# A low part, two GpSimd sums and one copy change places in a pipelined transformer kernel

## Time and profile before

| | |
|---|---|
| median of three runs | 924.88 us (922.01 to 927.58) |
| profiled execution | 921.48 us |
| its span, first to last instruction | 919.6 us |
| mean granted clock of PE | 0.966 of 2.4 GHz |
| busy: PE, DVE, ACT, POOL | 88%, 82%, 68%, 19% |
| a body, bodies 3 to 13 | 50.2 us |

### The profile page before, as it was taken

The page is one execution under the profiler, slowest core; times in us unless marked ns, Lnnn a source line. Parts: engine busy times, 40 slices in busy tenths (PEclk is TensorE's granted clock), DMA queues, the critical chain, the costliest instruction groups (busy, mean ns, idle before and its releaser), DMA issues.

```text
span 919.6 us, 18573 instructions
## 1 busy us (share of the span) xinstructions
PE 812.3 (88%) x5962; PEld 694.2 (75%) x5962; DVE 755.9 (82%) x2475; ACT 621.0 (68%) x1279; POOL 172.8 (19%) x160
## 2 busy tenths in 40 slices
PE   2276789999999999999999999999999999998782
PEld 0264668888889787888888888878888888787681
DVE  3648586798989989898989899898989898969565
ACT  1123668786868686877878686868788796777330
POOL 2100002121220403121212113030212121201110
PEclk9687899999999999999999999999999999999986
DMA  6714587667774757675686958486667657572100
GB/s 200 225 65 123 140 192 179 159 147 184 166 183 133 171 142 180 155 168 153 160 180 153 182 135 185 135 182 152 164 150 184 159 135 173 156 174 63 52 34 12
DMA packets 147737, 137.59 MB, mean 150 GB/s; under 512 B 19298, under 2 KB 144803, under 8 KB 147636
## 3 DMA queue, kind: packets, MB, share of 16 engines
q1 hardware_dynamic: 147636, 136.33, 60.6%
HBM read 98.49 MB, written 4.23 MB: 112 GB/s over the span
## 4 chain that ended last, share of the span: by engine, by line
PE 62%; ACT 18%; issue 8%; DVE 6%; SPq 4%; DMA 2%; POOL 1%; POOLq 0%; DVEq 0%; ACTq 0%
PE back_bank L1054 12%; PE turn_bank L1010 9%; PE context_bank L1064 6%; PE score_bank L1112 5%; PE front_bank L1048 5%; PE score_bank L1113 4%; ACT sc L529 4%; PE front_bank L1081 4%; ACT ffT L597 4%; PE back_bank L1034 3%; PE attend_bank L1034 3%; PE back_bank L1025 3%; PE front_bank L1218 2%; SPq L308 2%; ACT L529 2%
## 5 line engine op out<-in xcount | busy, mean ns | idle before, releaser
L529 ACT ACTIVATE sc<-sc,negmax 128x256 f32<-128x256 f32 x512 | 230.4, 500 | 39.0 <-DVE negmax L844 38.5
L844 DVE CUSTOM_DVE_ANT_0 sc<-score_bank,side 128x256 f32<-128x256 f32 x512 | 195.2, 419 | 37.9 <-PE score_bank L1113 34.1
L515 ACT ACTIVATE pt<-turn_bank 128x512 f32<-128x512 f32 x176 | 104.8, 595 | 134.7 <-PE turn_bank L1010 94.7
L1010 PE MATMUL turn_bank<-ident,sc 128*128 128x128 f32 x1024 | 157.2, 276 | 1.3 <-ACT sc L529 1.2
L1010 PEld LDWEIGHTS turn_bank<-ident,sc 128*128 128x128 f32 x1024 | 123.3, 141 | 32.3 <-issue 13.7
L452 POOL TENSOR_TENSOR rstd<-var,half_neg 128x2 f32<-128x2 f32 x64 | 54.3, 848 | 436.6 <-DVE var L773 435.3
L1112 PE MATMUL score_bank<-ks,qs 128*128 128x256 f32 x512 | 122.6, 321 | 8.0 <-DVE negmax L844 6.7
L1054 PE MATMUL back_bank<-w,ffT 128*128 128x256 f32 x512 | 118.0, 379 | 0.0
L1054 PEld LDWEIGHTS back_bank<-w,ffT 128*128 128x128 f32 x512 | 97.0, 190 | 12.7
L1113 PE MATMUL score_bank<-mask_neg,ident_r 128*128 128x512 f32 x256 | 102.1, 399 | 0.0
L1112 PEld LDWEIGHTS score_bank<-ks,qs 128*128 128x128 f32 x512 | 78.3, 192 | 16.7 <-DVE negmax L844 8.9
(11 more groups left out here) (209 smaller groups left out, 1990.0 us busy)
## 6 DMA issues: line engine op xcount, KB each, us to landing
side<-in_side SPq DMA_DIRECT2D x128, 512.0 KB, 5.1
qs<-qh SPq DMA_DIRECT2D x128, 64.0 KB, 4.2
ks<-kh SPq DMA_DIRECT2D x128, 64.0 KB, 3.8
ks<-kl SPq DMA_DIRECT2D x128, 64.0 KB, 4.3
qs<-ql SPq DMA_DIRECT2D x128, 64.0 KB, 4.4
wb<-in_wb SPq DMA_DIRECT2D x16, 512.0 KB, 6.7
xN<-in_x SPq DMA_DIRECT2D x16, 256.0 KB, 4.8
ada<-ada_rows SPq DMA_DIRECT2D x16, 256.0 KB, 4.9
```

The source lines that it names most:

```text
L515: e.activation(pt[:, h % NP2, :, :], two(tbank[h % 2]), ACT.Copy).then_inc(copied[h % 4], 1)
L529: i = e.activation(sc[:, h % NS, q, :], sc[:, h % NS, q, :], ACT.Exp, bias=negmax[:, q, h:h + 1], scale=-1.0)
L844: i = e.tensor_tensor_reduce(sc[:, s % NS, q, :], two(sbank[s % 2])[:, q, :], side[:, (H * X.i + s) % NSIDE, q, :], -1.0, 3.4e38, ALU.add, ...
L1010: i = e.transpose(tbank[h % 2][:, k * S + q * P:k * S + q * P + P], sc[:, h % NS, q, k * P:k * P + P], ident[:, :])
```

## The change

Four places change; no arithmetic does.

1. DVE: `u_l` (L856) moves from the end of slot 1 to slot 0, behind the bias of head 0 and ahead of the norm of layer 0 (L786, L794).
2. POOL: `x2b` (L487) moves from slot 13 of the body in which its sample is in B to slot 1 of the next (its sample is then in T), ahead of that slot's power. It waits for n3 and, where there is an F, for F's y.
3. POOL: `x1res` (L475) moves from slot 14 to slot 13, ahead of that slot's power, and waits for `xa` of G, where there is a G, as `x2b` did before.
4. ACT: in slot 13 the copy of turned head 11 moves ahead of the tanh. In bodies without B there is no tanh in this slot.

```diff
@@ -461,13 +461,20 @@
                         e.wait_ge(ready, 2 + SET0)
                     if is_step(t, s, 1, 0):
                         e.wait_ge(ready, 4 + SET0)
+                    if s == 1 and T:
+                        if F:
+                            e.wait_ge(ev["y_ready"], F.n)
+                        e.wait_ge(ev["n3_ready"], T.n)
+                        e.tensor_tensor(x2b[:, :, :], x2[:, :, :], rows(b2r[:, :]), ALU.add).then_inc(ev["x2b_ready"], 1)
                     if s == 1 and F:
                         power(F, 1, ev["y_var"], ev["y_rstd"])
                     if s == 4 and T:
                         e.wait_ge(ev["bcf_ready"], T.n)
                         e.wait_ge(ev["x3_turned"], T.n)
                         e.tensor_tensor(x3c[:, :, :], x3[:, :, :], rows(bcf[:, :]), ALU.add).then_inc(ev["x3c_ready"], 1)
-                    if s == 14 and F:
+                    if s == 13 and F:
+                        if G:
+                            e.wait_ge(ev["xa_ready"], G.n)
                         wait(e, ev["x2_ready"], F.i - 1)
                         e.wait_ge(ev["x1_ready"], F.n)
                         if t == -1:
@@ -480,11 +487,6 @@
                         power(T, 3, ev["x4_var"], ev["x4_rstd"])
                     if s == 8 and B:
                         power(B, 2, ev["x2_var"], ev["x2_rstd"])
-                    if s == 13 and B:
-                        e.wait_ge(ev["n3_ready"], B.n)
-                        if G:
-                            e.wait_ge(ev["xa_ready"], G.n)
-                        e.tensor_tensor(x2b[:, :, :], x2[:, :, :], rows(b2r[:, :]), ALU.add).then_inc(ev["x2b_ready"], 1)
                     if s == 13 and G:
                         power(G, 0, ev["xa_var"], ev["xa_rstd"])
                     if s == 15 and B:
@@ -605,6 +607,8 @@
                     if s == 12 and G:
                         e.wait_ge(ev["expert_done"], G.n)
                         e.activation(g1[:, :], fbank[:, 0:S], ACT.Identity, bias=wexp[:, A:A + 1]).then_inc(ev["g1_ready"], 1)
+                    if s == 13 and X:
+                        copy_turned(X, s - LT)
                     if s in (11, 12, 13, 14) and B:
                         j = s - 11
                         quarter(e, "u1_ready", B, j)
@@ -613,7 +617,7 @@
                         e.activation(th[:, j % 2, :, :], ffT[:, 2 * j:2 * j + 2, :], ACT.Tanh, scale=0.851).then_inc(ev["th_ready"], 1)
 
                     for x, h in lagging(X, B, s - LT):
-                        if s in ACT_COPIES:
+                        if s in ACT_COPIES and s != 13:
                             copy_turned(x, h)
 
             turns(body)
@@ -845,15 +849,15 @@
                                                        -1.0, 3.4e38, ALU.add, ALU.min, negmax[:, q, s:s + 1])
                         i.then_inc(biased[s % 4], 1)
 
+                    if s == 0 and U:
+                        e.wait_ge(ev["uh_ready"], U.n)
+                        e.tensor_tensor(u_l[:, :, :], t_u[:, :, :], u_h[:, :, :].bitcast(F32), ALU.subtract).then_inc(ev["ul_ready"], 1)
                     if s == 0 and F:
                         norm_scale(F, 0, xa, gamma0[:, :], ev["xa_rstd"], ev["y_scaled"])
                         norm_shift(F, 0, yN, xa, beta0[:, :], ev["y_scaled"], ev["y_ready"])
                     if s == 1 and F:
                         e.wait_ge(ev["y_ready"], F.n)
                         norm_stats(F, 1, yN, ev["y_stats"], ev["y_aggr"], ev["y_var"])
-                    if s == 1 and U:
-                        e.wait_ge(ev["uh_ready"], U.n)
-                        e.tensor_tensor(u_l[:, :, :], t_u[:, :, :], u_h[:, :, :].bitcast(F32), ALU.subtract).then_inc(ev["ul_ready"], 1)
                     if s == 2 and T:
                         e.wait_ge(ev["w2_done"], T.n)
                         e.wait_ge(ev["x2b_ready"], T.n)
```

## The result

The changed kernel takes 900.47 us (median of 4 runs, 899.63 to 902.63); the kernel before, beside it, took 924.75 (4 runs, 922.01 to 927.58). The ratio is 0.9741, 95% interval 0.9707 to 0.9775. The forecast was 900 from 924.88.

The account below looks back on a forecast made before the run. TensorE was taken to bound the kernel, with 1.51 us idle per full body. Gains of 17.3 (u_l), 5.5 (copy), 1.0 and 1.0 (sums at the ends) make 24.8 us, from 924.88 to a forecast of 900, range 893 to 909.

Parts of the forecast that it names:

- issue: Profile's label for TensorE's 1.20 us wait at differ, slot 2, 12 times; read as waiting for u_l, costing 1.44 each.
- full-body term of 1.82: Gain per full body: 1.44 us at differ from moving u_l, 0.38 at slot 14's mix from moving the copy.
- What is late next: Check of body 8, slot 14 through slots 2 to 10, with TensorE and VectorE earlier; claimed nothing binds.
- The sum would be the same: If GpSimd's multiply held L939 in slot 14, total gain unchanged; slot 4's margin shrinks from 0.9 to 0.4 us.
- Rival 2: New wait in slots 3 to 5 takes back about half of the 1.44 us: 908.8 us, 9 in 100.
- I take nothing for the new neighbours: Slot 1: bias of head 1 and statistics beside moved x2b counted as slowed by 0; bound 1.06 us.
- Body 15's 1.0: Gain of 1.0 us in body 15, as neither moved sum would block the norm at L794 there.
- The blocked scale in body 0: F's norm at 66.82, blocked by x1res, takes 1.89 us for 0.88; unblocking it was to win 1.0 us.
- Rival 1: The copy ahead of slot 13's tanh gives nothing at slot 14's mix: 905.6 us, 11 in 100.
- rival 3: Pause at differ in slot 2 stays, being TensorE's own: 917.4 us, 3 in 100.
- rival 4: TensorE's granted clock falls when it works without pauses; slower, 937 us at clock 0.94, 5 in 100.
- Rival 5: No change: pauses come back one for one on VectorE, 82% busy; 924 us, 2 in 100.

Follow-up runs that it names:

- low_copy: Against the kernel before, u_l moves to slot 0 and the copy ahead of the tanh, GpSimd's two sums stay: 923.51 us, ratio 0.9995.
- x1res_14: The changed kernel with the sum x1res alone put back in slot 14: 913.08 us, ratio 0.989 to the kernel before.
- low_only: Against the kernel before, only u_l moves to slot 0; sums and copy stay: 916.2 us, ratio 0.9942.
- clear_ends: The changed kernel with three more GpSimd waits: x3c for the x1 shift, x2b without F for u_l, x1res without G for f: 898.76 us, ratio 0.974.
- low_sums: The changed kernel with the copy of head 11 put back behind the tanh: 904.56 us, ratio 0.979 to the kernel before.
- sums_only: Against the kernel before, only GpSimd's two sums, x2b and x1res, move: 908.77 us, ratio 0.9859.

## Why the prediction was right, and which step of it was wrong

**Right: what bounds the kernel.** "1.51 us of a body is all that a better order can win there" counted idle time alone; with what each stall costs beyond its length (1.44 and 0.38 in all) the working gave 1.82, and 1.83 was measured. TensorE is then busy for the whole body, so this order has no idle time left to win. Reading "issue" as a wait for L856, from the timeline, was right: each kernel that writes `u_l` early enough, by whichever route, has no pause at `differ`.

**Right: the copy.** 0.38 a body with the others (48.76 to 48.37), nothing alone, since TensorE then only waits longer in slot 2. The copy ends at 494.24 and `mix` starts without a wait 0.43 later; with the 0.15 that it needs behind a copy the margin is 0.28, where the working had 0.06. ACT, then PE, body 8 of after (answers to rows 6 and 7):

```profile
493.63 0.61 ACT L517 ACTIVATE pt<-turn_bank 128x512 f32<-128x512 f32 x1
494.11 0.66 ACT L617 ACTIVATE th<-ffT 128x512 f32<-128x512 f32 x1
```

```profile
494.67 1.06 PE L1068 MATMUL context_bank<-pt,vp 128*18 128x256 f32 x16
```

**Wrong: "In the bodies at full load this buys no further time, as the end of `u_l` already left the path; it only widens margins."** Without the sums' move the same two edits buy nothing (low_copy: 50.22). The full-body term of 1.82 had the right size, but was put to two edits that reach it only together with the third: going from low_copy to the change, the sums' move is worth 1.85. The failed step is in "What is late next": it followed TensorE's steps and VectorE's steps, each moved earlier, and asked only which would wait for which. It did not ask what else TensorE's signals start. The turn of x3 starts `x3c` on GpSimd (in the earlier trace rows its releaser stands in the brackets: back_bank L995), and the shift of x1, two SBUF inputs, stood just ahead of it, in the timeline of VectorE before:

```profile
465.75 0.88 DVE L794 SCALAR_TENSOR_TENSOR x<-xa,rstd,ada 128x256 f32<-128x256 f32 x2
```

467.60 - 465.75 = 1.85, a margin of 0.97 beyond the shift's 0.88. Both numbers were there, and the rest is subtraction: with `u_l` early TensorE comes 1.44 sooner, gap 0.41 (measured 0.34); with the copy 1.82 sooner, gap 0.03 (measured 0.03); VectorE 1.06 earlier gives 1.09 (measured 1.05). The change is fast because 1.05 is more than 0.88, by 0.17 us. The cost of a collision was in the earlier trace rows too, 1.0 us. So the forecast number was right in part by luck, with a margin that it didn't know of. Rival 2 (9 in 100) named the right stretch; where it comes true, without the sums' move, its price was too small: 1.85 a body, not half of 1.44.

**Wrong for the same reason: "The sum would be the same", if L939 were held.** VectorE would then stay 1.06 late. x1res_14, where `x2b` has moved and L939 is held, is the nearest to that case and loses 1.23 a body (913.08); low_copy loses 1.85 (923.51). That case called for a rival from 913 up, and not for a thinner margin. A smaller slip: L939 was held in 12 bodies (2 to 13), not in 13; the 1.06 stands in no term of the sum.

**Right but for a little: "I take nothing for the new neighbours".** The bias and the statistics beside the moved sums kept their times. The small `var` operation behind the statistics takes 0.28 beside `x1res` in slot 13, where it takes 0.17 alone (before it took 0.34 there, beside `x2b`).

**The page's rule and the row.** After the change GpSimd's multiply starts at 496.68, as foreseen just ahead of the tanh's reader. VectorE beside it:

```profile
496.73 0.68 DVE L943 SCALAR_TENSOR_TENSOR ffT<-th,ffT 128x512 f32<-128x512 f32 x1
497.33 0.88 DVE L827 TENSOR_TENSOR x<-fN,grid_c 128x512 f32<-128x512 f32 x1
```

L943 takes its plain 0.68 (mean 686 ns over all 64) and the next two-input operation 0.20 more. But the multiply doesn't go free: it takes 1.45 here, and 0.93 in bodies 14 to 16, where no two-input operation of VectorE stands at its start (in body 15 one starts 0.33 behind it, and both keep their plain times). GpSimd in body 15:

```profile
821.08 0.93 POOL L494 TENSOR_SCALAR bcr<-bcr,flags 128x256 f32<-128x256 f32 x1 [5.58 <-DMA bcr<-in_bc]
```

In the kernel before it took 1.88, beside the held L939 and L823; the prediction read the plain 0.68 of L823 there and not the length of the multiply. So the two do get in each other's way, and here it is GpSimd that pays, 0.52. The Trainium skill (SBUF — State Buffer, "Who interferes with whom") has whoever issues first keep the shared pair for the whole instruction. For the multiply this case's trace doesn't agree as recorded: it starts 0.05 us ahead of L943, and by the rule it would be L943 that waits. For the sums it agrees in part: in low_only `x3c` starts in the first half of the shift, and the second half takes 1.51 us, until 0.28 after the sum has ended. The other way round, in body 2 of after, the sum starts 0.43 after the shift, by when its second half is under way, and it is GpSimd that is longer (1.60 for 1.29); GpSimd, then VectorE:

```profile
172.39 1.60 POOL L474 TENSOR_TENSOR x<-x,bcr 128x512 f32<-128x512 f32 x1 [3.42 <-PE back_bank L999]
```

```profile
171.96 0.88 DVE L798 SCALAR_TENSOR_TENSOR x<-xa,rstd,ada 128x256 f32<-128x256 f32 x2
```

In low_copy it doesn't agree: the shift is recorded 0.03 ahead of the sum, and yet its first half takes 1.60 for 0.48 and the sum its plain 1.29. Where the two starts lie within 0.05 us, the recorded order doesn't tell who waits; what decides it stays open.

**The ends.** Body 15's 1.0 came, though "in body 15 neither comes" wasn't so: `x2b` stands on the edge operation there (1.28 for 0.37, 0.45 us by clear_ends). The blocked scale in body 0 (66.82, 1.89) takes 0.88 now. From the start of `xa` to the end of the shift VectorE needs 4.70 in body 0, for 5.60 before, and TensorE's wait for the bias there falls from 1.99 to 0.56. In the length of the bodies this can't be seen: over all eleven kernels body 0 lasts 49.3 to 52.5 and body 1 41.6 to 43.1, whether the sums moved or not, as TensorE's clock changes level in this stretch. Whether that 1.0 reaches the end stays open. In body 16 `x2b` does hit the shift of f (1.87 for 0.88), taken as 0 with a bound of 0.4. The 0 was right: in clear_ends the shift takes 0.86, and VectorE then stands idle for 1.05 waiting for ScalarE's `n3h`, as the prediction had it.

**Rivals.** Rival 1 (the copy gives nothing) is refuted by low_sums, rival 3 (the pause isn't removed) by low_only, rival 4 (the clock) by the granted 1.00 in body 8. Rival 5 (pauses come back one for one on VectorE) is what low_copy does, without the sums' move.

## What to carry to other kernels

When one engine is made faster, list every instruction that its signals start, on third engines too, and subtract: a GpSimd sum that starts 1.8 us sooner can land on a two-input VectorE operation and give the whole gain back. Edits that look like they serve one stall (here all three: the low part, the copy, the sums) have values that depend on each other: alone they are worth 0.43, 0 and 1.14 us a body, together 1.83; try them together before one is dropped. Subtract on the ends of the program too, where small operations can stand beside a moved sum. And a margin found afterwards, here 0.17 us, is as much part of the result as the time.

## What had not been expected of the hardware

- The price of a collision between a GpSimd sum of 128 x 512 and a VectorE operation in two halves goes in steps with the start: 0.03 us into the operation 1.47 (both halves late), 0.13 and 0.34 into it 1.03 (the second half; at 0.13 GpSimd is 0.2 longer as well), at 0.43 none for VectorE and 0.3 for GpSimd. The steps come from x1res_14, low_only, low_copy and body 2 of after.
- GpSimd's TENSOR_SCALAR of 128 x 256 takes 0.93 where no two-input VectorE operation stands at its start, and 1.45 where one starts 0.05 behind it; that one loses nothing and the next 0.20. In sums_only, body 14, it is the other way round: the tanh's reader starts 0.09 behind it and takes 0.92, and the multiply its 0.93.
- A stall of TensorE costs more than its length. The wait of 0.31 ahead of `mix` cost 0.38 (48.76 and 48.37; 46.87 and 46.50), the one of 1.20 ahead of `differ` 1.44 (1.20 + 1.19 before, 0.94 after, is 1.45).
